# Batch 0's keys and queries laid out in two halves of head pairs, with padding written by memset and batch 1's query split placed between the first maxima

## The chip, the cores and the metric

The kernel runs on one core of a Trainium2 chip, as one program in which five engines work from their own queues and meet only through semaphores: TensorE (PE, with its weight loads PEld), VectorE (DVE), ScalarE (ACT), GpSimd (POOL) and SyncE (SP, which here only issues DMAs). The metric is device time in microseconds. Before the change the median of three runs is 338.34 us (338.0 to 339.09).

## The reference, cut to what matters

Four layers on `x` [4, 256, 128] with a context `ctx` [4, 512, 64]: self-attention plus cross-attention, a routed mixture of experts, a second cross-attention, a second mixture.

```python
x = x + tanh(g_xattn[0]) * L0_xattn(layernorm(x), ctx)   # the change lies in here
x = x + tanh(g_ffn[0])   * L0_ffn(layernorm(x))          # 8 experts, top 2, limited capacity
x = x + tanh(g_xattn[1]) * L1_xattn(layernorm(x), ctx)
x = x + tanh(g_ffn[1])   * L1_ffn(layernorm(x))

def L0_xattn(x, c):                                      # H = 16 heads of width 8
    q, k, v = heads(x @ Wq + bq), heads(x @ Wk + bk), heads(x @ Wv + bv)
    y  = softmax(causal(q @ k.T / sqrt(8))) @ v          # 256 queries on 256 keys
    qc, kc, vc = heads(x @ Wcq + bcq), heads(c @ Wck + bck), heads(c @ Wcv + bcv)
    y += softmax(qc @ kc.T / sqrt(8)) @ vc               # 256 queries on 512 context keys
    return merge(y) @ Wp + bp
```

## The kernel before, in words

**Parts and products.** A head has width 8, so one product would fill 8 of TensorE's 128 rows. Each float32 query and key is therefore cut into three bfloat16 parts (high, middle, low; tile `parts`, one row for each of the 128 channels) and six products of parts are laid side by side in the rows of two tiles, `qcat` and `kcat` (128 rows x batch x 8 head pairs x columns). In these a group of 64 rows holds one head of a pair; row r of every eight rows holds product r for r = 0 to 5, rows 6 and 7 of every eight are padding: ones in `kcat`, and in `qcat` zeros with the maxima of the scores put into some of them later. Query columns are 256 self and 256 cross (QW = 512); key columns 256 self and 512 context (KW = 768). `every(cat, b, r)` names the 16 rows r, r + 8, ... of batch b. One DMA fills one product of one batch: 16 rows x 8 pairs from 128 rows of `parts`. The weights are permuted first (`permute`), so that the projected channels come out in the order (parity, channel, pair) in which these copies need them.

**The lead.** For batch 0 the order on VectorE is written by hand: statistics of x tiles 0 and 1, permuting the weights, normalising, statistics of tiles 2 and 3, then `split` of the context keys, the queries, the self keys (high part, rest, middle part, low part: four operations each), with normalisations between, and the query split of batch 1. GpSimd takes the power -0.5 of the variances (`rstd_group`, lines 668 and 669) for the tile groups (0,1), (2,3), (4 to 7), then makes 14 constants in a row, then subtracts for batches 1 to 3 (line 720 for the remainder, 727 for the low part), with ScalarE casting between (`take_high` line 820, `split_middle` line 817). The projections are `jobs`: ct and xt (transposes of context and x), q, k, ck (keys of the context), v, cv. TensorE computes job j into a PSUM bank, ScalarE copies it out in the same order. `unread_zeros` are filler products on TensorE that nobody reads.

**Pass 1** computes the score maxima: eight parts (batch, half of the head pairs) of 11 units each: 8 "cross" (line 1583), 2 "late" (1585), 1 "early" (1588). VectorE reduces each unit (line 1174, two banks of 512 columns). After part n the maxima are split in three (GpSimd `split_max`, lines 710 to 713), turned by TensorE (1548), copied (1152) and brought into `qcat` by DMAs (`max_rows`, line 600). **Pass 2** computes the scores again with the maxima subtracted (lines 1607 to 1612), exponentiates on ScalarE (911) and multiplies by the values (1641). The first 18 steps of pass 1 run ahead of pass 2, each with one projection job behind it on TensorE.

**SyncE's queue** in order: the loads of x, context and weights; `pad(0)`; batch 0's context keys, three of the six query copies (ScalarE issues the other three), the self keys; seven small loads; `lay_out_batch(1)` and `pad(1)`; then for each part its `max_rows`, with batch 2 behind part 0's and batch 3 and the last pads behind part 1's.

## Time and profile before

| | us |
|---|---|
| median of 3 runs | 338.34 (338.0 to 339.09) |
| span of the profiled execution | 334.4 |
| PE busy in the span | 312.3 (93%) |
| DVE busy | 223.1 (67%) |
| ACT busy | 195.2 (58%) |
| POOL busy | 116.6 (35%) |
| first unit of pass 1 on TensorE | 19.50 |
| first scores of pass 2 on TensorE | 42.58 |

The profiled execution's time outside its span is not listed; the median of the runs stands 3.9 us above the span. The page's chain that ended last gives TensorE 67% of the span, VectorE 8%, SyncE's queue 5%, ScalarE 5%, GpSimd 5%. The granted TensorE clock has a mean of 1.00. In a timeline row stand start, length, engine, line, operation, output<-input, count, and in brackets the idle time ahead of it with what ended it; operations that follow one another on one line are merged, and a merged row's length runs from the first start to the last end.

### The profile page before, as it was taken

Reading aid. Unit: us, or ns where it says so; the run is one execution under the profiler, and the core shown is the slowest. Engines: PE = TensorE matmul, PEld = TensorE weight load, DVE = VectorE, ACT = ScalarE, POOL = GpSimd, SP = SyncE. Lnnn points to the kernel's source line nnn. Section 1 sums busy time; section 2 is a strip of 40 time slices with the busy share of each in tenths; the row PEclk is TensorE's granted clock in tenths of the full one; section 3 lists DMA queues with packets and bytes.
Section 4 is the critical chain, followed back from the end, with each engine's and each line's share of the span. In section 5 each row is a group of like instructions: output and inputs, shape, how many; then the busy total and the mean of one; then the engine's idle time right before and its main releaser. Section 6 shows DMA issues by size and latency. Waiting matters only on the chain.

```text
span 334.4 us, 7547 instructions
## 1 busy us (share of the span) xinstructions
PE 312.3 (93%) x2909; PEld 190.8 (57%) x2911; DVE 223.1 (67%) x537; ACT 195.2 (58%) x417; POOL 116.6 (35%) x209
## 2 busy tenths in 40 slices
PE   8778969989999999999989999999997899999995
PEld 3435733444444444354478677777795367676665
DVE  4998798888989898866544052333331957779665
ACT  3448588888889988867468633323336256422221
POOL 6476732325532343214477103444442211110000
PEclk9999999999999999999999999999999999999999
DMA  7956895950419005160081372000003100000101
GB/s 171 207 110 165 173 214 124 210 102 3 161 45 274 7 2 154 41 194 1 18 236 41 94 210 66 20 18 22 20 13 92 50 2 0 3 0 0 33 1 31
DMA packets 35827, 27.83 MB, mean 83 GB/s; under 512 B 5627, under 2 KB 33070, under 8 KB 35792
## 3 DMA queue, kind: packets, MB, share of 16 engines
q1 hardware_dynamic: 33965, 25.04, 30.0%
q0 software_dynamic: 1280, 1.88, 1.8%
q10 hardware_dynamic: 547, 0.44, 0.5%
q8 instruction: 23, 0.38, 0.5%
q14 instruction: 12, 0.10, 0.1%
HBM read 11.89 MB, written 5.26 MB: 51 GB/s over the span
## 4 chain that ended last, share of the span: by engine, by line
PE 67%; DVE 8%; SPq 5%; ACT 5%; POOL 5%; issue 5%; DMA 3%; DVEq 0%; ACTq 0%; POOLq 0%
PE psum L1835 11%; PE psum L1641 10%; PE psum L1916 8%; PE psum L1904 4%; PE psum L1823 4%; PE psum L1583 4%; PE psum L1607 3%; DVE nmax L1174 2%; SPq L544 2%; PE psum L1659 2%; POOL rows_in L773 2%; PE psum L2019 2%; PE psum L1610 2%; PE psum L2011 1%; PE psum L1773 1%
## 5 line engine op out<-in xcount | busy, mean ns | idle before, releaser
L1174 DVE TENSOR_REDUCE nmax<-psum 128x2 f32<-128x1024 f32 (+2 forms) x88 | 103.1, 1213 | 13.1 <-PE psum L1583 8.4
L911 ACT ACTIVATE parts<-psum 128x512 f32<-128x512 f32 (+1 forms) x88 | 45.2, 568 | 8.4 <-PE psum L1607 8.0
L1835 PE MATMUL psum<-p_more,kcat 128*128 128x320 f32 (+2 forms) x160 | 40.2, 396 | 0.9 <-DVE p_more L1305 0.7
L795 POOL DMA_INDIRECT rows_back<-qcat,back_at x24 | 22.9, 953 | 46.3 <-ACT qcat L944 40.3
L1835 PEld LDWEIGHTS psum<-p_more,kcat 128*128 128x128 f32 x160 | 26.1, 190 | 9.1 <-issue 0.9
L1309 DVE TENSOR_TENSOR qcat<-psum,qk_r 128x320 f32<-128x320 f32 (+2 forms) x40 | 16.7, 422 | 21.1 <-ACT qk_r L952 21.0
L952 ACT ACTIVATE qk_r<-psum 128x320 f32<-128x320 f32 (+2 forms) x40 | 15.3, 384 | 24.1 <-PE psum L1835 22.8
L1641 PE MATMUL psum<-parts,v_aug 128*9 128x256 f32 (+1 forms) x352 | 28.2, 366 | 0.0
L1916 PE MATMUL psum<-h_t,kcat 128*128 128x512 f32 x60 | 28.1, 594 | 0.0
L1641 PE MATMUL psum<-qk_r,v_aug 128*9 128x256 f32 (+1 forms) x160 | 27.1, 370 | 0.0
L990 ACT ACTIVATE qk_r<-psum 128x512 f32<-128x512 f32 x15 | 9.0, 597 | 30.1 <-PE psum L1916 30.1
L1583 PE MATMUL psum<-kcat,qcat 64*128 64x512 bf16 x128 | 24.9, 386 | 1.7 <-DMA qcat<-parts 1.7
L1607 PE MATMUL psum<-qcat,kcat 64*128 64x256 bf16 x256 | 24.7, 271 | 1.9 <-ACT p_more L911 0.8
L1641 PE MATMUL psum<-qk,v_aug 128*9 128x256 f32 (+1 forms) x160 | 25.8, 360 | 0.0
L1305 DVE COPY p_more<-psum 128x320 f32<-128x320 f32 x8 | 3.9, 492 | 28.1 <-PE psum L1813 28.1
L911 ACT ACTIVATE qk_r<-psum 128x512 f32<-128x512 f32 (+1 forms) x40 | 20.8, 574 | 2.0 <-PE psum L1607 1.8
L911 ACT ACTIVATE qk<-psum 128x512 f32<-128x512 f32 (+1 forms) x40 | 20.0, 551 | 1.9 <-PE psum L1607 1.9
L1583 PEld LDWEIGHTS psum<-kcat,qcat 64*128 64x128 bf16 x128 | 6.1, 92 | 24.4 <-issue 12.6
L1904 PEld LDWEIGHTS psum<-kcat,qcat 128*128 128x128 f32 x120 | 15.6, 191 | 6.4 <-issue 5.0
L773 POOL DMA_INDIRECT rows_in<-h_rows,put_at x16 | 15.9, 996 | 7.3 <-issue 4.4
L934 ACT ACTIVATE kcat<-psum 128x512 f32<-128x512 f32 x24 | 12.6, 616 | 8.3 <-PE psum L1773 8.3
L1358 DVE TENSOR_TENSOR qcat<-psum,qk_r 128x512 f32<-128x512 f32 x15 | 10.3, 690 | 9.5 <-ACT qk_r L990 9.5
(247 smaller groups left out, 627.2 us busy)
## 6 DMA issues: line engine op xcount, KB each, us to landing
kcat<-parts SPq DMA_DIRECT2D x18, 192.0 KB, 3.8
qcat<-parts SPq DMA_DIRECT2D x21, 128.0 KB, 3.6
kcat<-ones_b SPq DMA_DIRECT2D x8, 192.0 KB, 4.7
kcat<-in_L_ffn_wi_gate_dram SPq DMA_DIRECT2D x6, 256.0 KB, 4.3
kcat<-in_L_ffn_wi_up_dram SPq DMA_DIRECT2D x6, 256.0 KB, 4.6
kcat<-in_L_ffn_wo_dram SPq DMA_DIRECT2D x6, 256.0 KB, 5.4
parts<-in_L_ffn_w_dram SPq DMA_DIRECT2D x3, 512.0 KB, 5.5
rows_in<-zeros SPq DMA_DIRECT2D x1, 1290.0 KB, 6.2
```

The lines of the kernel that those rows point to most:

```text
L773: pool.indirect_dma_start(out=rows_in[0:E * SLOTS, :], out_offset=bass.IndirectOffsetOnAxis(ap=put_at[:, k, t:t + 1], axis=0), in_=h_rows[ ...
L795: pool.indirect_dma_start(out=rows_back[:, :], out_offset=bass.IndirectOffsetOnAxis(ap=back_at[0:m, e, t:t + 1], axis=0), in_=eo[0:m, e % ...
L911: act.activation(p_slots[u % NPT][:, 0:w], s2_bank(s2_place[u])[:, 0:w], ACT.Exp, scale=SCALE).then_inc(p_in, 1)
L952: act.activation(sg[:, i % 2, 0:m], gate_up_bank(i, 0)[:, 0:m], ACT.Silu).then_inc(sg_in[0], 1)
L1174: dve.tensor_reduce(dst[:, :, n * g:n * (g + 1)], src.rearrange("p (r q k) -> p r q k", r=PAR, q=n), AX.X, ALU.max, negate=True).then_inc( ...
L1309: dve.tensor_tensor(hh[:, e % 2, f, first:end], gate_up_bank(i, 1)[:, 0:end - first], sg[:, i % 2, 0:end - first], ALU.mult).then_inc(hh_i ...
L1583: ins = pe.matmul(dst, q[:, S + t * P:S + (t + 1) * P], k[:, S:KW], start=True, stop=True)
L1607: ins = pe.matmul(dst[:, c * S:(c + 1) * S], k[:, key:key + P], q[:, S:QW], start=True, stop=True)
L1641: ins = pe.matmul(bank(o_bank(n))[32 * j:32 * j + HA, cols], v_aug[:, v, h, :], p, start=r in (0, 2), stop=r in (1, ROUNDS - 1), skip_grou ...
L1835: ins = pe.matmul(gate_up_bank(i, m)[:, 0:end - first], w_t[e][:, m, f * P:(f + 1) * P], xs_t[:, e % 2, first:end], start=True, stop=True)
L1904: ins = pe.matmul(bank(DN_BANK[n % 4])[:, t * P:(t + 1) * P], hh1[:, n % 2, t * P:(t + 1) * P], w1_t[:, e, 2, :], start=True, stop=True)
L1916: ins = pe.matmul(bank(2 + 2 * (i % 2) + m), w1_t[:, e, m, :], h_t[:, s * BANK:(s + 1) * BANK], start=True, stop=True)
```

## The change

Batch 0's head pairs are laid out in two halves: pairs 0 to 3 first (all that part 0 of pass 1 reads), pairs 4 to 7 behind them, 18 copies of their own. For this batch 0 needs another channel order, (half, row, pair), so its weights are permuted by VectorE into a place of their own (`w_first`, `b_first`, inside `p_more`), and GpSimd permutes once more, in the order (row, pair), for batches 1 to 3. The padding of batch 0 is no longer copied by DMA: GpSimd sets the whole of batch 0's `kcat` to ones and VectorE the whole of its `qcat` to zeros before the copies. The statistics of tiles 2 and 3 move behind the split of the context keys. The query split of batch 1 is cut in two and stands behind the second and the fourth unit of pass 1 on VectorE; the clearing of bank 7 goes behind the fourteenth. `pad(1)` and the value weights are issued early on SyncE, and half of batch 1's copies go behind part 0's `max_rows`.

```diff
@@ sync @@
-            def lay_out_batch(b):
+            def lay_out_batch(b, first, end):
                 sp.wait_ge(parts_in, b + 1)
...
             sp.wait_ge(zero_in, 2)
-            pad(0)
+            pad(1)
+            sp.dma_start(w_v[:, :], a["L0_xattn_Wv"]).then_inc(in_wv, 16)
+            sp.dma_start(w_cv[0:DC, :], a["L0_xattn_Wcv"]).then_inc(in_wv, 16)
+            sp.dma_start(w_cv[DC:DC + 1, :], a["L0_xattn_bcv"].unsqueeze(0)).then_inc(in_wv, 16)
+            sp.wait_ge(ones_set, 1)
             sp.wait_ge(early_in, 1)
-            for dst, src in lay_out_k(0, S, KW):
+            for dst, src in first_k(0, S, KW):
                 sp.dma_start(dst, src).then_inc(cat_in[0], 16)
             sp.wait_ge(early_in, 2)
-            for dst, src in list(lay_out_q(0))[:Q_ON_SP]:
+            for dst, src in list(first_q(0))[:Q_ON_SP]:
                 sp.dma_start(dst, src).then_inc(cat_in[0], 16)
             sp.wait_ge(parts_in, 1)
-            for dst, src in lay_out_k(0, 0, S):
+            for dst, src in first_k(0, 0, S):
                 sp.dma_start(dst, src).then_inc(self_in, 16)
+            for pieces in (first_k(1, S, KW), first_q(1), first_k(1, 0, S)):
+                for dst, src in pieces:
+                    sp.dma_start(dst, src).then_inc(second_in, 16)
...
-            lay_out_batch(1)
-            pad(1)
+            lay_out_batch(1, 0, NPROD // 2)
...
                 if n == 0:
-                    lay_out_batch(2)
+                    lay_out_batch(1, NPROD // 2, NPROD)
+                    lay_out_batch(2, 0, NPROD)
@@ gpsimd @@
             rstd_group(0, *groups_of(0)[0])
-            pool.wait_ge(h_in[0], QT)
+            pool.memset(kcat[:, 0].rearrange("p a n -> p (a n)").bitcast(F32), TWO_ONES).then_inc(ones_set, 1)
+            rstd_group(0, *groups_of(0)[1])
+            pool.wait_ge(in_wq, 16 * N_IN_WQ)
+            permute(b_perm[:, :], b_rows)
+            for m, w in enumerate((w_q, w_cq, w_k)):
+                permute(w_perm[:, m, :], w)
+            pool.wait_ge(in_wck, 16 * N_IN_WCK)
+            permute(w_perm[0:DC + 1, 3, :], w_ck)
+            pool.wait_ge(perm_in, 5)
             const(pool.memset(c_t[DC:DC + 1, SC:NC * P], 1.0))
-            for first, end in groups_of(0)[1:]:
-                rstd_group(0, first, end)
+            rstd_group(0, *groups_of(0)[2])
@@ vector @@
+            dve.memset(q_zero[:, 0:Q_SET], 0.0)
             dve.wait_ge(in_x[0], 16)
             statistics(0, 0, x_sb)
...
+            dve.memset(q_zero[:, Q_SET:PAIR * QW // 2], 0.0)
             normalise(0, 0, x_sb)
...
-            dve.wait_ge(in_x[1], 16)
-            statistics(0, 1, x_sb)
...
             split(0, QW + S, XW, False)
+            dve.wait_ge(in_x[1], 16)
+            statistics(0, 1, x_sb)
             normalise(0, 1, x_sb)
...
-            dve.wait_ge(job_act, taken_count(job_at("q", SPLIT_DVE)))
-            split(SPLIT_DVE, 0, QW, False)
...
+                if i == SPLIT_AFTER[0]:
+                    split_cast(SPLIT_DVE, 0, QW)
+                if i == SPLIT_AFTER[1]:
+                    split_rest(SPLIT_DVE, 0, QW)
+                if i == SPLIT_AFTER[2]:
+                    wait_taken(dve, max(j for j in range(len(jobs)) if job_bank[j] == O_BANK))
+                    dve.memset(bank(O_BANK), 0.0).then_inc(o_clear, 1)
@@ tensor @@
                 if kind == "xt":
+                    if i == 1:
+                        pe.wait_ge(perm_in, 1)
+                        pe.transpose(dst[:, S:S + 3], b_perm[:, :], ident[0:3, 0:3])
...
-                        pe.wait_ge(perm_in, 1)
-                    ins = pe.matmul(dst, w_perm[0:DC + 1, 3, :],
+                        pe.wait_ge(perm_first, 1)
+                    else:
+                        pe.wait_ge(perm_in, 5)
+                    ins = pe.matmul(dst, (w_perm if i else w_first)[0:DC + 1, 3, :],
...
                     pe.wait_ge(cat_in[b], 16 * 2 * NPROD)
-                    pe.wait_ge(pad_in[b], 16 * 4)
+                    if b > 0:
+                        pe.wait_ge(pad_in[b], 16 * 4)
+                    if part == 1:
+                        pe.wait_ge(second_in, 16 * 3 * NPROD)
```

`SPLIT_AFTER` is (1, 3, 13), counted from 0. On TensorE the projection of the context keys of batch 1 waits, before and after, for GpSimd's memset of `c_t` (semaphore `consts`, value 4), and GpSimd's low part of batch 1 waits for the end of the query split (`early_in`, value 3).

VectorE's queue from the first normalisation to the statistics of tiles 4 to 7, before (`w_ck`, `w_q`, ... are weights, `qk` and `qk_r` the float32 values and the remainder):

```order
L1086 TENSOR_SCALAR h_rows<-x_sb,ln_mv,ln_rstd 128x128 x2
L1067 COPY b_perm<-b_rows 3x128
L1067 COPY w_perm<-w_q 128x128
L1067 COPY w_perm<-w_cq 128x128
L1067 COPY w_perm<-w_k 128x128
L1078 BN_STATS ln_stats<-x_sb 128x6 x2
L1081 BN_AGGR ln_mv<-ln_stats 128x2 x2
L1105 CAST parts<-qk 128x512
L1106 TENSOR_TENSOR qk_r<-qk,parts 128x512
L1112 CAST parts<-qk_r 128x512
L1113 TENSOR_TENSOR parts<-qk_r,parts 128x512
L1086 TENSOR_SCALAR h_rows<-x_sb,ln_mv,ln_rstd 128x128 x2
```

The same stretch of VectorE's queue after the change, from the first weight copy on:

```order
L1108 COPY p_more<-b_rows 3x128
L1108 COPY p_more<-w_q 128x128
L1108 COPY p_more<-w_cq 128x128
L1108 COPY p_more<-w_k 128x128
L1160 CAST parts<-qk 128x512
L1161 TENSOR_TENSOR qk_r<-qk,parts 128x512
L1167 CAST parts<-qk_r 128x512
L1168 TENSOR_TENSOR parts<-qk_r,parts 128x512
L1119 BN_STATS ln_stats<-x_sb 128x6 x2
L1122 BN_AGGR ln_mv<-ln_stats 128x2 x2
L1127 TENSOR_SCALAR h_rows<-x_sb,ln_mv,ln_rstd 128x128 x2
```

The statistics pair has moved from ahead of the four split operations to behind them, directly ahead of the normalisation of the same tiles; the copies write to `p_more`.

GpSimd's queue over the three `rstd` groups, before:

```order
L668 TENSOR_SCALAR ln_rstd<-ln_mv 128x2
L669 TENSOR_TENSOR ln_rstd<-ln_rstd,half_neg 128x2
L678 MEMSET c_t 1x1536
L668 TENSOR_SCALAR ln_rstd<-ln_mv 128x2
L669 TENSOR_TENSOR ln_rstd<-ln_rstd,half_neg 128x2
L668 TENSOR_SCALAR ln_rstd<-ln_mv 128x4
L669 TENSOR_TENSOR ln_rstd<-ln_rstd,half_neg 128x4
```

GpSimd's queue over the same stretch after:

```order
L698 TENSOR_TENSOR ln_rstd<-ln_rstd,half_neg 128x2
L710 MEMSET kcat 128x3072
L697 TENSOR_SCALAR ln_rstd<-ln_mv 128x2
L698 TENSOR_TENSOR ln_rstd<-ln_rstd,half_neg 128x2
L706 COPY b_perm<-b_rows 3x128
L706 COPY w_perm<-w_q 128x128
L706 COPY w_perm<-w_cq 128x128
L706 COPY w_perm<-w_k 128x128
L706 COPY w_perm<-w_ck 65x128
L719 MEMSET c_t 1x1536
L697 TENSOR_SCALAR ln_rstd<-ln_mv 128x4
L698 TENSOR_TENSOR ln_rstd<-ln_rstd,half_neg 128x4
```

The memset of `kcat` stands where that of `c_t` stood; five copies and the memset of `c_t` now stand between the second and the third group.

## Rows read from the trace of the kernel before

**Rows 1.** Chain that ended last, 0 to 76 us: start, length, what

```profile
14.52 1.13 POOL ln_rstd L669
...
21.24 1.65 POOL qk_r L720
...
51.49 0.78 SPq L600
...
67.07 0.77 SPq L600
```

**Rows 2.** VectorE's timeline, 0 to 46 us

```profile
1.18 0.27 DVE L1090 MEMSET zeros<- 128x258 f32 x1
...
3.69 0.25 DVE L1081 BATCH_NORM_AGGREGATE ln_mv<-ln_stats 128x2 f32<-128x6 f32 x2
...
5.11 0.61 DVE L1086 TENSOR_SCALAR h_rows<-x_sb,ln_mv,ln_rstd 128x128 f32<-128x128 f32 x2 [1.02 <-POOL ln_rstd L669]
5.62 0.25 DVE L1067 COPY b_perm<-b_rows 3x128 f32<-3x128 f32 x1
...
7.17 0.49 DVE L1078 BATCH_NORM_STATS2 ln_stats<-x_sb 128x6 f32<-128x128 f32 x2 [0.77 <-DMA x_sb<-in_x_dram]
...
10.07 0.60 DVE L1086 TENSOR_SCALAR h_rows<-x_sb,ln_mv,ln_rstd 128x128 f32<-128x128 f32 x2
...
11.04 0.69 DVE L1106 TENSOR_TENSOR qk_r<-qk,parts 128x512 f32<-128x512 f32 x1
...
12.84 0.86 DVE L1078 BATCH_NORM_STATS2 ln_stats<-x_sb 128x6 f32<-128x128 f32 x4
13.74 0.38 DVE L1081 BATCH_NORM_AGGREGATE ln_mv<-ln_stats 128x2 f32<-128x6 f32 x4
...
17.23 0.77 DVE L1106 TENSOR_TENSOR qk_r<-qk,parts 128x512 f32<-128x512 f32 x1
...
19.94 8.08 DVE L1174 TENSOR_REDUCE nmax<-psum 128x2 f32<-128x1024 f32 x7 [0.16 <-PE psum L1583]
```

**Rows 3.** ScalarE's timeline, 0 to 46 us: the context keys of batch 0

```profile
6.56 0.60 ACT L871 ACTIVATE qk<-psum 128x512 f32<-128x512 f32 x1 [1.22 <-PE psum L1519]
```

**Rows 4.** TensorE's timeline, 0 to 45 us

```profile
13.05 1.02 PE L1519 MATMUL psum<-c_t,w_perm 65*128 65x512 f32 x2
...
16.75 0.44 PE L1498 MATMUL psum<-ident,h_rows 128*128 128x128 f32 x2 [1.38 <-DVE h_rows L1086]
...
19.50 0.39 PE L1583 MATMUL psum<-kcat,qcat 64*128 64x512 bf16 x2 [1.67 <-DMA qcat<-parts]
...
27.05 1.10 PE L1509 MATMUL psum<-h_t,w_perm 128*128 128x256 f32 x4 [0.85 <-ACT h_t L850]
...
33.70 0.40 PE L1574 MATMUL psum<-mask_w,ident_w 64*128 64x128 bf16 x8
...
37.26 0.29 PE L1548 MATMUL psum<-ident_w,nmax_p 128*48 128x128 bf16 x2
```

**Rows 5.** GpSimd's timeline, 0 to 46 us

```profile
2.43 0.74 POOL L662 MEMSET ones_b<- 128x768 bf16 x1
...
5.77 1.95 POOL L678 MEMSET c_t<- 1x1536 f32 x1 [0.70 <-DVE h_rows L1086]
...
15.98 0.29 POOL L682 CAST ident_w<-ident 128x128 bf16<-128x128 f32 x1
...
23.83 1.64 POOL L727 TENSOR_TENSOR parts<-qk_r,parts 128x768 bf16<-128x768 f32 x1 [0.95 <-ACT parts L817]
...
26.71 2.61 POOL L720 TENSOR_TENSOR qk_r<-qk,parts 128x1280 f32<-128x1280 f32 x1 [1.24 <-ACT parts L820]
```

**Rows 6.** SyncE's queue, 0 to 78 us

```profile
16.03 3.92 SPq L556 DMA_DIRECT2D kcat<-parts  x6
...
47.26 0.61 SPq L544 DMA_DIRECT2D kcat<-parts  x1
```

**Rows 7.** DMA issues, 0 to 45 us: count, KB each, us to landing

```profile
kcat<-parts SPq DMA_DIRECT2D x6, 64.0 KB, 2.9
```

## What is predicted, before the changed kernel was run

> **What bounds the kernel now.** I read the 40 slices and the granted clock first (1.00 from end to end, so TensorE runs at its 2.4 GHz level and the clock is no term here), then the chain that ended last over the first 76 us, then each engine's timeline over the same stretch. The change ends there: behind 76 us nothing is edited, and most of the chain is TensorE in step with its own queue, so a shift at 76 us reaches the end nearly whole.
>
> In the chain [rows 1] the reader is to see that the lead is not bound by the first maxima. The path goes VectorE statistics of tiles 4 to 7 (end 14.12) -> GpSimd's rstd (ends 15.65) -> GpSimd's constants, without a gap -> GpSimd's first subtraction for batch 1 (21.24) -> ScalarE, whose projections of batch 2 stand behind the middle part of batch 1 -> TensorE's query projection of batch 3 at 27.05. From there TensorE has no gap in its timeline until past the first turn of the maxima at 37.26 [rows 4]; later the chain holds SyncE, issuing without a rest from 51.49 to 67.07. The first maxima start at 19.50 when the last query copy lands, 1.67 us after TensorE was ready. So an earlier landing alone pays nothing: the wait at 27.05 is made by GpSimd.
>
> **The change, part by part.**
>
> *Statistics moved behind the first split (VectorE).* From 7.17 to 14.12 VectorE worked without a gap: 6.95 us [rows 2]. The new order does the same work, but tiles 2 and 3 get their statistics directly ahead of their normalisation, so GpSimd's rstd is now waited for with nothing between. What that costs stands at the first group: statistics end 3.94, normalisation starts 5.11, 1.17 us. Before, the split hid it. In exchange VectorE need not wait for the x tiles at 7.17; the context keys are there at 7.1 [rows 3] and the copies are done at 6.40.
>
> *Padding by memset.* Two memsets of qcat on VectorE (1536 and 512 words): at 1.06 ns a word (258 words in 0.27 us [rows 2]) I estimate 1.6 and 0.55 us, which fall into its idle times ahead of the first statistics (1.45 to about 3.2, as 0.5 us of statistics stand ahead of the row at 3.69) and ahead of 5.11 (1.02 us), cost 0. The memset of kcat on GpSimd, 3072 words: 768 elements took 0.74 us [rows 5], four times that is 2.96, less three fixed parts, so 2.8 us, from 5.1 to 7.9. It starts as the first normalisation does, and ahead of VectorE's four weight copies (5.62 to 6.4). The question on which most hangs is who waits. GpSimd's 1536-word memset at 5.77 met these very copies and took 1.95 us; by the 768-element row it should take about 1.4, and the excess is near the 0.6 us of the copies: the two do exclude each other. The other way round there is one small row: a VectorE subtraction at 17.23, started while GpSimd had a select under way, took 0.77 us against 0.69 at 11.04 [rows 2]. Bounds: the copies are not held (0), or they are held until 7.9 (2.3 us). I take the second, since here GpSimd is first. Then the copies end at 8.7, and the split of the context keys starts at 8.7 instead of 7.1.
>
> The Trainium skill ("SBUF — State Buffer", Who interferes with whom) says that the port pair which VectorE's two-port copies and GpSimd share is locked for a whole instruction and that whoever comes first keeps it. The trace shows GpSimd as the loser, with 0.6 us; that VectorE loses for 2 us no row here shows. By that rule alone the sum is the one I take.
>
> *The sum to the statistics of tiles 4 to 7.* Held: 8.7 + 6.95 + 1.17 = 16.8. Not held: 7.1 + 6.95 + 1.17 = 15.2. Before: 14.12. So +2.7 or +1.1.
>
> *GpSimd behind it.* The second rstd ends 2.9 + 1.17 us after the split starts (7.17 to 10.07 is the 2.9): 12.8 held, 11.2 not. Then it has five new permuting copies (a contiguous 128x128 cast took 0.29 [rows 5]; with a gap 0.35 each, 1.7 us; strided they may cost twice that) and the 1536-word memset, 1.4 us, moved behind them; VectorE's casts (0.4 us, as between 10.67 and 11.04) hold them up, each once, 0.9 us taken. Together 4.0 us (bounds 3.1 to 6): 16.8 or 15.2, just when the statistics are there, so no more is added. Third rstd 1.5 us, constants 5.5 us as before (15.65 to 21.24), less some 0.2 since the batch 1 casts no longer meet them: the subtraction for batch 1 starts at about 23.8 or 22.2, +2.5 or +0.9.
>
> *Start of the maxima.* Half layouts carry half the bytes but are issued one for one: 0.65 us each [rows 6]. With the query split done 1.28 us before the statistics (12.84 to 14.12), the last query copy is issued 1.3 us later and lands about 2.9 us on for 64 KB [rows 7]: 19.7 or 18.1. But TensorE's context-key projection of batch 1 now waits for the memset that moved, until 16.8 or 15.2, and from it to the first maximum are 2.32 + 1.08 us of its own queue (13.05 to 15.37, 16.75 to 17.83 [rows 4]), plus the rstd wait of tiles 4 and 5 inside these: 20.3 or 18.7, against 19.50.
>
> *The batch 1 split between maxima.* About 2.3 us, as the same four operations took for batch 0 (10.6 to 12.84), leave VectorE before the maxima and come back in two halves behind the second and fourth. TensorE's seventh unit needs five reduces (8.08 / 7 = 1.154 each): 0.4 + 5 x 1.154 + 2.3 = 8.5 us after the first, and the unit itself takes 0.4, so the projection at 27.05 could go at about 29.2 or 27.6; GpSimd's road gives 29.55 or 27.95. Both ends meet. GpSimd's second subtraction for batch 1 (23.83 before) now waits for the fourth maximum and the rest of the split, 27.6 or 26.0, takes 1.64, and batch 2's (26.71) stands behind it: 29.3 or 27.7, so +2.6 or +1.0; GpSimd's road from there leads to the first turn of the maxima (37.26). I carry +2.6 and +1.1.
>
> *SyncE's queue.* Ahead of the first maximum of part 1 (33.70) now stand six self keys and eighteen second-half copies: from 18.3, 24 x 0.65, last landing 36.2 (33.3 + 2.9), where TensorE arrives at 33.70 + 2.5 = 36.2. Cost 0, up to 1 if one issue is long. Six batch 1 copies now follow the first row of maxima: SyncE was free at 47.87 and the next turn came at 51.49; 6 x 0.65 = 3.9 brings it to 51.75, both plus the shift: +0.3, and this is on the chain until 67.07.
>
> *At nothing:* the value weights loaded early (SyncE idled there), ones and zeros of batch 1 sent first, the second bias transpose (0.2 us on TensorE in its filler stretch), ScalarE's wait for the padding.
>
> Sum held: 2.6 + 0.3 = **+2.9 us**: span 334.4 to 337.3, and with the 3.9 us by which the median 338.34 stands above that span, 341.2. The profiled execution's own total isn't shown, so I hang the shift on the median.
>
> **Rivals.**
> 1. *GpSimd's memset gives way* and the copies run at 5.62. 1.1 + 0.3 = +1.4: 339.7 (339.2 to 340.6). For it: every large stretch in the trace is GpSimd's. Against: there it came second or had little to write.
> 2. *No measurable change.* The delay is eaten: the GpSimd constants run 0.6 shorter, and the SyncE term is nought; 338.0 to 339.3. Against: TensorE has no gap from 27.05 on.
> 3. *Faster.* The maxima start early and GpSimd reaches batch 1 before 21.24. It decides at the third rstd: it must start before about 14.2, that is, the 1.17 us must be hidden. Then at most the 0.85 us gap at 27.05 goes, 338.3 - 0.85 - 0.3 for shorter GpSimd constants: 337.2. Against: the wait is in the order of VectorE's own queue.
> 4. *Second halves late*: issues longer than 0.65 us or a landing beyond 2.9: +1 more, 342.3.
>
> **How the numbers follow.** Held 0.42, with late halves 0.08 (own range together 340.6 to 342.6); rival 1 0.27; no change 0.13; faster 0.10. Within 0.3% means 337.3 to 339.4, which takes a tenth of rival 1 too. So faster 0.10, same 0.17, slower 0.73. The range 339.2 to 342.5 leaves out the two last cases and a little above.
>
> **What would show it.** Held: the first weight copy on VectorE starts or ends near 7.9, not 5.8; the split of the context keys starts at 8.7. Either way: a gap of about 1.2 us ahead of the normalisation of tiles 2 and 3; GpSimd's first batch 1 subtraction after 22; TensorE's batch 3 query projection near 29.5 (held) or 28; SyncE busy without a gap from about 18 to 36 and again from 41 to 69. I am wrong if batch 1's subtraction starts by 21.3, or if a gap in TensorE's queue between 27 and 42 us swallows the delay.

## The result, and the profile after

The changed kernel takes 2.35% longer: the ratio to the kernel before is 1.0235, interval 1.0194 to 1.0276. A second comparison, on a chip where the kernel before takes about 345 us, gave 1.0261 (1.0213 to 1.0309). On the first ratio and 337.99 us for before in the first comparison, this is 345.9 us. The median as measured, 350.33 us, is no better number: three of the six runs took 345.0 to 346.3 us and three 354.3 to 354.9 at a lower granted clock, and before had only the first kind there. The profiled execution took 344.97 us, span 343.2 against 334.4: 8.8 us, where 2.9 were forecast.

The page of the changed kernel; digits are tenths, the clock's too:

```profile
span 343.2 us, 7577 instructions
PE 317.8 (93%) x2912; PEld 193.2 (56%) x2912; DVE 229.2 (67%) x539; ACT 195.7 (57%) x418; POOL 120.1 (35%) x215
...
PEclk9696999999999999999999999999999999999999
```

The clock was no term in the forecast. Here it falls twice inside the first 35 us, and nowhere else before the end.

VectorE of the changed kernel (start, length, what, and in brackets the idle time ahead with what ended it); it answers to [rows 2]:

```profile
5.09 2.72 DVE L1127 TENSOR_SCALAR h_rows<-x_sb,ln_mv,ln_rstd 128x128 f32<-128x128 f32 x2 [0.47 <-POOL ln_rstd L698]
7.74 0.25 DVE L1108 COPY p_more<-b_rows 3x128 f32<-3x128 f32 x1
...
8.44 0.41 DVE L1160 CAST parts<-qk 128x512 bf16<-128x512 f32 x1
...
11.19 0.25 DVE L1122 BATCH_NORM_AGGREGATE ln_mv<-ln_stats 128x2 f32<-128x6 f32 x2
12.59 0.78 DVE L1127 TENSOR_SCALAR h_rows<-x_sb,ln_mv,ln_rstd 128x128 f32<-128x128 f32 x2 [1.15 <-POOL ln_rstd L698]
...
23.68 1.81 DVE L1147 CAST parts<-qk 128x512 bf16<-128x512 f32 x1
25.52 0.69 DVE L1148 TENSOR_TENSOR qk_r<-qk,parts 128x512 f32<-128x512 f32 x1
26.25 2.36 DVE L1227 TENSOR_REDUCE nmax<-psum 128x2 f32<-128x1024 f32 x2
28.52 0.42 DVE L1153 CAST parts<-qk_r 128x512 bf16<-128x512 f32 x1
28.97 0.69 DVE L1154 TENSOR_TENSOR parts<-qk_r,parts 128x512 bf16<-128x512 f32 x1
```

GpSimd beside it, to [rows 5]:

```profile
5.01 2.66 POOL L710 MEMSET kcat<- 128x3072 f32 x1
...
23.57 1.64 POOL L760 TENSOR_TENSOR qk_r<-qk,parts 128x768 f32<-128x768 f32 x1
29.81 1.64 POOL L767 TENSOR_TENSOR parts<-qk_r,parts 128x768 bf16<-128x768 f32 x1 [4.61 <-DVE parts L1154]
31.40 2.60 POOL L760 TENSOR_TENSOR qk_r<-qk,parts 128x1280 f32<-128x1280 f32 x1
```

Two things of VectorE end only just after one of GpSimd's, though no semaphore joins them: the normalisation at 7.81, the memset at 7.67 (2.72 us, 0.61 before), and the cast at 25.49, the subtraction at 25.21 (1.81, the next one 0.42). Batch 2's subtraction starts at 31.40, 4.7 us later than before.

TensorE over the same stretch, to [rows 4]:

```profile
20.98 0.39 PE L1653 MATMUL psum<-kcat,qcat 64*128 64x512 bf16 x2
...
27.53 0.39 PE L1653 MATMUL psum<-kcat,qcat 64*128 64x512 bf16 x2 [1.90 <-DVE nmax L1227]
...
30.86 0.61 PE L1653 MATMUL psum<-kcat,qcat 64*128 64x512 bf16 x2 [0.59 <-DVE nmax L1227]
31.39 2.07 PE L1574 MATMUL psum<-h_t,w_perm 128*128 128x256 f32 x4
```

The projection of batch 3 comes 4.3 us late and takes 2.07 us, not 1.10. Last, ScalarE, and the chain from SyncE's last copy of batch 2 to it:

```profile
62.65 1.08 ACT L952 ACTIVATE parts<-psum 128x512 f32<-128x512 f32 x2 [3.27 <-DMA kcat<-parts]
```

```profile
44.66 0.86 SPq L628
...
56.27 0.61 SPq L569
56.92 5.71 DMA kcat<-parts
62.65 1.08 ACT parts L952 x2
```

ScalarE writes its exponentials where batch 2's split keys and queries lie, so it must wait until these are copied out. Before, the last of the copies was issued at 47.26 [rows 6] and nobody waited; now it is the row at 56.92, issued 9.7 us later, and it lands 5.7 us on.

So the 8.8 us stand in two places. The start of the second pass (the first scores for the exponentials, once the first maxima rows have landed) goes from 42.58 to 48.49: 5.9. From its fifth step on it is 3 us more (64.77 against 55.85): the 3.27 of ScalarE's wait. The ninth step is at 79.65 against 71.40, which is 8.25, since the kernel before waits there for a row of maxima (4.6 us from its eighth step, 4.0 after the change). From 167 us on the two are 8.6 to 8.8 apart.

### The profile page after: what moved, and what is told of

Read it like the earlier page. It is cut to its first block, busy times and chain, and to the rows that moved or that the text cites. A ratio compares the mean times of both kernels' runs of the same rounds, so it can differ in the third digit from the quotient of the medians.

```text
span 343.2 us, 7577 instructions
## 1 busy us (share of the span) xinstructions
PE 317.8 (93%) x2912; PEld 193.2 (56%) x2912; DVE 229.2 (67%) x539; ACT 195.7 (57%) x418; POOL 120.1 (35%) x215
## 4 chain that ended last, share of the span: by engine, by line
PE 64%; DVE 11%; POOL 6%; ACT 5%; DMA 5%; issue 5%; SPq 3%; DVEq 0%; ACTq 0%; POOLq 0%
PE psum L1711 11%; PE psum L1905 11%; PE psum L1986 8%; POOL rows_in L813 4%; PE psum L1653 4%; PE psum L1974 4%; PE psum L1893 4%; PE psum L1677 4%; SPq L569 3%; DVE nmax L1227 3%; PE psum L1729 2%; ACT parts L952 2%; PE psum L2089 2%; DVE h_rows L1127 2%; PE psum L1680 2%
## 5 line engine op out<-in xcount | busy, mean ns | idle before, releaser
L1653 PE MATMUL psum<-kcat,qcat 64*128 64x512 bf16 x128 | 25.6, 396 | 2.6 <-DVE nmax L1227 2.6
L1677 PEld LDWEIGHTS psum<-qcat,kcat 64*128 64x128 bf16 x256 | 10.6, 94 | 13.0 <-ACT parts L952 4.3
```

Source lines behind the costliest of these rows:

```text
L1653: ins = pe.matmul(dst, q[:, S + t * P:S + (t + 1) * P], k[:, S:KW], start=True, stop=True)
L1677: ins = pe.matmul(dst[:, c * S:(c + 1) * S], k[:, key:key + P], q[:, S:QW], start=True, stop=True)
```

## The experiments

Chips differ, so the table gives places in each profiled execution, in us, and the ratio to before on the same chip where there is one. Behind the first comparison four more were made, each on its own chip: of copies_back, split_back, ones_by_dma and all_three (the kernel before took 343.5 us there at the least); of after_repeat, before_repeat, stats_alone and shared_alone (343.6); of memset_alone and mended (336.4); of mended_whole and before_qset (335.8). The only traces of the kernel before are the first and before_repeat. "Norm. 2" is the start of VectorE's second normalisation, "stats" the end of the statistics of tiles 4 to 7, "b2" GpSimd's subtraction for batch 2, "turn" the first turn of the maxima, "pass 2" and "9th" the first and ninth step of the second pass.

| kernel | norm. 2 | stats | b2 | turn | pass 2 | 9th | ratio |
|---|---|---|---|---|---|---|---|
| before | 10.07 | 14.12 | 26.71 | 37.26 | 42.58 | 71.40 | 1 |
| before_repeat | 10.83 | 15.37 | 27.98 | 38.53 | 43.85 | 73.17 | |
| changed | 12.59 | 17.17 | 31.40 | 43.17 | 48.49 | 79.65 | 1.0235 |
| after_repeat | 12.40 | 17.00 | 31.25 | 43.53 | 48.85 | 79.97 | 1.0261 |
| copies_back | 12.63 | 17.21 | 31.44 | 42.98 | 49.70 | 79.88 | |
| split_back | 12.57 | 17.16 | 29.75 | 40.25 | 45.57 | 77.62 | 1.0114 |
| all_three | 11.52 | 16.11 | 28.70 | 39.23 | 52.40 | 83.32 | |
| stats_alone | 12.09 | 16.14 | 28.74 | 39.29 | 44.60 | 73.77 | 1.0064 |
| shared_alone | 10.05 | 14.09 | 29.56 | 39.98 | 45.82 | 75.12 | 1.0092 |
| memset_alone | 11.90 | 15.94 | 28.53 | 39.08 | 44.39 | 73.26 | 1.0022 |
| mended | 11.01 | 15.58 | 28.19 | 38.70 | 44.02 | 76.66 | 1.0120 |
| mended_whole | 11.03 | 15.61 | 28.21 | 38.71 | 44.03 | 72.72 | 1.0005 |
| before_qset | 10.19 | 14.24 | 28.87 | 39.41 | 44.73 | 73.45 | 0.9975 |

**Undoing one part of the change.** Three edits of the changed kernel, and all of them together. With the split the clearing of bank 7 goes back too.

```
copies_back:  -lay_out_batch(1, 0, NPROD // 2)       +lay_out_batch(1, 0, NPROD)
              -lay_out_batch(1, NPROD // 2, NPROD)    (behind the first maxima row)
split_back:   +split(SPLIT_DVE, 0, QW, False)         (ahead of the maxima, as before)
              -split_cast(...)  -split_rest(...)       (between the maxima)
ones_by_dma:  -pool.memset(kcat[:, 0]..., TWO_ONES)
              -pad(1) at the front   +pad(1) behind batch 1's first copies
              +sp.dma_start(every(kcat, 0, r), ones_b[:, :])   for the two rows
all_three:    the three together
```

> All six copy pairs of batch 1 stand ahead of the first row of maxima on SyncE again; everything else as in the changed kernel. Theory (three separate prices): in the changed kernel SyncE idles from 40.3 to 44.7 us, the six moved copies then push batch 2's last copy to a landing at 62.6, and ScalarE waits 3.3 us for it (its exponentials overwrite batch 2's parts). The moved copies fit into the idle time, so that wait goes or falls under 0.5 us, pass 2 still starts near 48.5, and the kernel takes 342.3 us (fast runs of the changed one: 345.6). Rival (the halves themselves cost, 18 copies more in the queue and on the DMA engines): ScalarE's wait stays above 2 us and the time at 345 to 346.

> The query split of batch 1 and the clearing of bank 7 stand ahead of the first maxima on VectorE again. Theory: GpSimd's 768-column subtraction (23.6 to 25.2) no longer holds a VectorE cast for 1.4 us between two maxima, TensorE's gaps of 1.9 us at 27.5 and 0.6 at 30.9 go, and with them the fall of the granted clock to 0.52 in 30 to 35 us; pass 2 starts at 45.5 to 46.5 instead of 48.5, ScalarE's wait for batch 2's copies stays, the kernel takes 343 us. Rival (the loss between maxima is only the moved 2.3 us, and moving it back puts the same 2.3 us ahead of the first maximum): pass 2 still at 48 to 48.5, 345 to 346 us.

> The ones of batch 0 come by two DMAs (as before the change) instead of GpSimd's memset of 3072 words; the zeros are still set by VectorE; the last pads of batch 1 go behind its first six copies. Theory: VectorE's first normalisation takes 0.6 us instead of 2.7, the context-key split starts at 7.1 instead of 8.4, TensorE's clock stays above 0.9 in 5 to 15 us, the statistics of tiles 4 to 7 end near 15.0 instead of 17.2, pass 2 starts near 46, and the kernel takes 343 us. Rival (VectorE's lateness comes from the moved statistics and the new copies on GpSimd, not from the memset): pass 2 at 48 and 345 us or more.

> The three edits together, so that what is left of the change is the halves, the two channel orders, the moved statistics and the early pads and weights. Theory: the prices are nearly independent, pass 2 starts at 43.5 to 44, no ScalarE wait, clock 1.00 throughout, 339 us, 1.0 to 1.4 us above the kernel before for the exposed rstd wait. Rival (the halves cost): pass 2 at 45 or later and 341 us or more.

split_back did what it should: turn and second pass 2.9 us earlier, ScalarE's wait as before (3.19). Its ratio, 1.0114 (1.0039 to 1.019), is against 1.0235 on the first chip. In copies_back ScalarE's wait is gone, but the first row of maxima now stands behind the six copies in SyncE's queue, and TensorE waits for it:

```profile
49.70 0.28 PE L1679 MATMUL psum<-qcat,kcat 64*128 64x256 bf16 x2 [1.77 <-DMA qcat<-nmax_t]
```

In all_three the turn is early, at 39.23, yet TensorE waits 8.2 us, because SyncE reaches the row only at 47.08, behind all twelve copies of batch 1 and the four of `pad(1)`; the second pass came at 52.40, not at the 43.5 to 44 that I expected:

```profile
46.43 0.61 SPq L563 DMA_DIRECT2D qcat<-zeros  x1
47.08 0.86 SPq L629 DMA_DIRECT2D qcat<-nmax_t  x1
```

ones_by_dma took the hold away (normalisation 0.60 us), but won only 0.66 us at the second normalisation, which went to 11.93, and the statistics ended at 16.52, not near 15.0. Its clock then stayed at half from 30 to about 65 us and its second pass began at 58.5, ratio 1.0617 (1.0511 to 1.0722); its times behind 27 us decide nothing.

The whole times of copies_back and all_three missed what I expected by far more: at the least 363.9 and 354.2 us, where I had 342.3 and 339. In both traces TensorE's clock is at about half from 200 to 220 us (0.53 and 0.50), far behind the edit, so these times price no part of the change, and no ratio stands for them.

**The same two kernels again, on a second chip.** Nothing is edited.

> The changed kernel, unedited, a second time, for a comparison with the kernel before on this chip and a second trace. If its two levels of time come from the kernel's own gaps (theory: VectorE's and GpSimd's holds in the lead, then a lowered TensorE clock), its trace has the same instruction starts up to the first lowered stretch: normalisation 2.7 us from 5.1, third unit of maxima held till about 23.6, second pass at 48 to 50, and ScalarE's 3.3 us wait on batch 2's last copy near 62. If the loss was that one chip's doing, the landmarks move back towards those of before (normalisation 0.61 us, second pass at 42.6) and the ratio falls to 1.00. Expected ratio 1.015 to 1.03.

> The kernel before, unedited, for a trace from this chip. Runs of it that are not profiled took from 343.5 to 359.1 us in the preceding comparison and 336.2 to 339.1 in the first. If the late lowered clock (between 180 and 225 us in three of the edited kernels, behind waits of TensorE ahead of the expert weights' transposes) belongs to the edits, this trace is at 2.4 GHz there; if it belongs to this chip, the same waits stand in it. The lead should be as in the first trace: second pass at 42.6 us.

The places of the changed kernel repeat within 0.4 us: the loss is the kernel's. The kernel before begins 1.3 us later here than in its first trace, since the two matmuls of TensorE's first context-key projection take 2.07 us together, not 1.13 (at a granted clock that still reads 1.00 there), and ScalarE's keys end at 8.54, not 7.16. So a single trace of the lead is good to about that; in shared_alone and before_qset, which have the same lead, the second normalisation starts at 10.05 and 10.19 as in the first trace. before_repeat also has late waits and a late fall of the clock (0.83 from 195 to 205 us) as the edited kernels do, so these don't need the change; a fall as deep as in all_three no trace of the kernel before shows.

```profile
186.13 3.10 PE L1774 MATMUL psum<-ident,parts 128*128 128x128 f32 x24 [2.01 <-issue]
```

**One part of the change alone, in the kernel before.**

```
stats_alone:   -dve.wait_ge(in_x[1], 16); statistics(0, 1, x_sb)   (ahead of the context keys' split)
               +the same two behind split(0, QW + S, XW, False)
shared_alone:  batch 1's split taken out ahead of the maxima and put behind maxima 1 and 3,
               counted from 0, as the changed kernel has it (bank 7 cleared behind the fourteenth)
memset_alone:  +link(pool.memset(kcat[:, 3]...[:, 0:3072], 0.0))   (behind the first rstd)
```

> The kernel before with one part of the change alone: the statistics of the second pair of tiles of batch 0 are moved behind the split of the context keys. Theory: the wait of 1.17 us for GpSimd's root, hidden behind the split before, stands open; the second normalisation goes from 10.07 to 11.2, the statistics of tiles 4 to 7 end at 15.2 instead of 14.12, the first unit of maxima at 20.3 instead of 19.5, and the second pass between 42.6 and 43.8. Rival: TensorE's own work there (the context transposes) covers it, and the maxima start at 19.5 unchanged.

> The kernel before with one part of the change alone: the split of batch 1's queries is taken out of its place ahead of the maxima and put in halves behind the second and the fourth maxima. Theory (splitting it there delays the chain of splits that TensorE's projections wait for): the first cast is held by GpSimd's subtraction or comes at 22 instead of 19, the q-projection of batch 3 goes from 27.05 to 29 to 30, the first turn from 37.26 to about 40, the second pass from 42.58 to about 45.5 (+2.9, as undoing it in the changed kernel took 2.9 off). Rival (it only costs behind a late lead): maxima start earlier, nothing is late, second pass within 0.5 of 42.58. As recorded ahead of the result: +2.6 at the turn.

> The kernel before with one thing added: behind its first root GpSimd fills 128 x 3072 words of kcat's fourth batch (which nobody reads before its own copies overwrite it) with zeros, in the place where the changed kernel has its memset of ones. Theory (held): VectorE's first normalisation lasts until the memset ends, 2.7 us instead of 0.61; the copies, the bias transposes and the q-projection of batch 0 move from 5.6, 6.1 and 7.5 to 7.7, 8.5 and 9.6; but the wait for ScalarE's eviction of the context keys ahead of the first split covers most of it, so the second normalisation is only 0.5 to 1 us late (10.6 to 11.1 instead of 10.07), the statistics of tiles 4 to 7 end at 14.7 to 15.1, GpSimd's own constants move with them, and the second pass starts 0.5 to 1.0 us late, at 43.1 to 43.6. As recorded (hold behind moved statistics): 1.6 us between held and not held. Rival (gives way): 0.6 us, nothing moves.

ScalarE's keys and VectorE of stats_alone:

```profile
7.22 0.60 ACT L871 ACTIVATE qk<-psum 128x512 f32<-128x512 f32 x1 [1.21 <-PE psum L1519]
```

```profile
7.85 0.43 DVE L1103 CAST parts<-qk 128x512 bf16<-128x512 f32 x1 [1.41 <-ACT qk L871]
...
10.62 0.25 DVE L1081 BATCH_NORM_AGGREGATE ln_mv<-ln_stats 128x2 f32<-128x6 f32 x2
12.09 0.60 DVE L1086 TENSOR_SCALAR h_rows<-x_sb,ln_mv,ln_rstd 128x128 f32<-128x128 f32 x2 [1.23 <-POOL ln_rstd L669]
```

The moved statistics cost 2.0 us in this trace, not the 1.2 that I expected, and the second pass came at 44.60, not by 43.8. The split starts at 7.85 in both traces, but for two reasons. Here it waits for ScalarE's keys, which end at 7.82. In the first trace of before they end at 7.16 [rows 3], and the split stands behind the statistics till 7.85. So in their old place the statistics cover keys that come up to 0.7 us late; moved, their own 0.8 us count, and the 1.23 us wait besides. With keys at 7.16 that is about 1.3 us (an estimate: 2.0 less the 0.7 that the keys came later), with keys at 7.82 it is 2.0. The ratio, 1.0064 (1.004 to 1.0087), is 2.2 us (1.4 to 3.0): about the whole shift reaches the end. The clock is 1.00 in this trace up to 180 us.

shared_alone, VectorE and GpSimd:

```profile
22.59 0.42 DVE L1107 CAST parts<-qk 128x512 bf16<-128x512 f32 x1
...
27.12 0.69 DVE L1114 TENSOR_TENSOR parts<-qk_r,parts 128x512 bf16<-128x512 f32 x1
```

```profile
20.50 1.64 POOL L721 TENSOR_TENSOR qk_r<-qk,parts 128x768 f32<-128x768 f32 x1
27.96 1.64 POOL L728 TENSOR_TENSOR parts<-qk_r,parts 128x768 bf16<-128x768 f32 x1 [5.82 <-DVE parts L1114]
29.56 2.61 POOL L721 TENSOR_TENSOR qk_r<-qk,parts 128x1280 f32<-128x1280 f32 x1
```

GpSimd's first subtraction is even 0.7 us earlier than before, and it gains nothing: it waits 5.8 us for VectorE's second half. +2.85 at batch 2, +3.2 at the second pass, ratio 1.0092 (1.005 to 1.0134), which is 3.2 us (1.7 to 4.6). In this trace the clock is at half from 20 to 25 us, so the 2.85 is not the sharing's alone. before_qset, further down, has the split in its old place and the same stretch at half clock, and its batch 2 subtraction comes at 28.87, 2.2 us late as well:

```profile
28.87 2.61 POOL L721 TENSOR_TENSOR qk_r<-qk,parts 128x1280 f32<-128x1280 f32 x1 [3.28 <-ACT parts L821]
```

In shared_alone VectorE stood idle for 0.9 us between its first four reduces, waiting for scores that TensorE computed at the low clock, which leaves about 2 us for the sharing (an estimate from those gaps). That it costs something in the kernel before rests on the ratio, and by it the rival, that it costs only behind a late lead, falls.

memset_alone shows the hold by itself, and a second one behind it:

```profile
5.05 2.72 DVE L1087 TENSOR_SCALAR h_rows<-x_sb,ln_mv,ln_rstd 128x128 f32<-128x128 f32 x2 [1.01 <-POOL ln_rstd L669]
...
9.06 1.01 DVE L1106 CAST parts<-qk 128x512 bf16<-128x512 f32 x1
...
11.90 0.60 DVE L1087 TENSOR_SCALAR h_rows<-x_sb,ln_mv,ln_rstd 128x128 f32<-128x128 f32 x2
```

It cost 1.8 us at the second normalisation and at the second pass, against the first trace of before from another chip, more than the 0.5 to 1 I expected. 1.2 us are the copies' delay (the split starts at 9.06, not 7.85), and 0.6 come from a second hold: GpSimd's other memset, one partition of 1536 words, now runs from 7.90 to 9.78 and holds the cast (1.01 us, 0.39 before). The ratio, 1.0022 (0.9992 to 1.0052), bounds the whole at 1.8 us and doesn't tell it from none.

**The changed kernel mended, with the halves and without.**

```
mended:        +pool.wait_ge(h_in[0], QT)             (ahead of the memset of ones)
               statistics(0, 1, x_sb) back ahead of the split; split_back's edit
mended_whole:  as mended, with lay_out_k(0, ...), lay_out_q(0) for first_k(0, ...), first_q(0);
               -for pieces in (first_k(1, S, KW), first_q(1), first_k(1, 0, S))
               VectorE permutes as before; and copies_back's edit
```

> The changed kernel with its three VectorE and GpSimd edits mended and its layout in halves kept: GpSimd's memset of ones waits for the first normalisation, the statistics of the second pair of tiles are back ahead of the context keys' split, batch 1's queries are split ahead of the maxima. The six copies of batch 1 stay behind the first maxima rows. Theory (the lead's loss is these three): normalisation 0.61, second normalisation at 10.1 to 10.9, statistics of tiles 4 to 7 end at 14.1 to 15.0, second pass at 42.6 to 43.6, five to six us earlier than in the changed kernel; ScalarE's 3 us wait on batch 2's last copy stays, since SyncE's eighteen more copies stay, so the whole is 2 to 4 us over before on this chip, ratio 1.005 to 1.012. Rival (the halves themselves are what costs): second pass at 46 or later. Rival (the halves bring something): first maxima before 19.3 and the ratio under 0.997.

> The mended kernel of the preceding run with batch 0 laid out whole again: every copy of batch 0 takes 128 partitions, the eighteen second-half copies are gone from SyncE's queue, and the six copies of batch 1 are back ahead of the first maxima rows. Kept are the memsets in place of batch 0's padding, GpSimd's copies of the weights and the early loads of the value weights. Theory (the halves' eighteen copies on SyncE are the rest of the loss): ScalarE's wait of 3.4 us on batch 2's last copy is gone, the second pass still begins at 43 to 44.5 and without a wait on the maxima rows, the ninth step of the second pass at 72 to 73.5 instead of 76.7, the ratio to before 0.998 to 1.005 where mended had 1.012. Rival (the wait comes from batch 1's late copies or from the shared traffic, not from the number of copies): the wait stays over 2 us, or one of more than 1 us appears ahead of the second pass, and the ratio stays at 1.01. The first unit of maxima may come later than 19.4, since whole copies take 2.9 to 3.8 us to land where halves took 1.9 to 2.1: at 19.5 to 20.5.

Mended, the second pass starts at 44.02, 4.5 us earlier than in the changed kernel but behind the 43.6 that I had at the latest (the later memset now holds a cast for 1.22 us), and the ratio is still 1.012 (1.0067 to 1.0172), because ScalarE's wait stays:

```profile
58.28 1.09 ACT L953 ACTIVATE parts<-psum 128x512 f32<-128x512 f32 x2 [3.38 <-DMA kcat<-parts]
```

With batch 0 laid out whole it is gone, at the same second pass to 0.01 us:

```profile
55.19 1.09 ACT L948 ACTIVATE parts<-psum 128x512 f32<-128x512 f32 x2 [0.28 <-PE psum L1668]
```

The ninth step is 3.9 us earlier and the ratio 1.0005 (0.9975 to 1.0035). This edit takes away the eighteen second-half copies and moves the six of batch 1 at once. copies_back moved the six alone, and there ScalarE's wait went too, but the row of maxima came late in its place: with eighteen copies more in the queue, one of the two waits stays in every run that keeps the halves. The first maximum came at 19.37 with the halves and at 20.30 without, and both kernels reached the turn at 38.70: the halves do bring the maxima forward, and that is worth nothing. SyncE's queue tells why whole copies suffice; in mended_whole batch 1 is out by 35.7 us, four us ahead of the row of maxima, where in mended only six of its twelve copies were:

```profile
35.10 0.61 SPq L568 DMA_DIRECT2D kcat<-parts  x1
39.62 0.86 SPq L624 DMA_DIRECT2D qcat<-nmax_t  x1
```

**The hidden part by itself.** The kernel before, with the padding of batch 0's queries filled by VectorE in place of two copies.

```
 before_qset:  -pad(0)   +its two copies of ones alone
               +dve.memset(q_zero[:, 0:Q_SET], 0.0) and the rest behind the first weight copy
```

> The kernel before with the one part of the change that stood in no busy stretch: the padding of batch 0's queries is filled by two VectorE memsets ahead of the first statistics (1.34 us) and behind the first copy of the weights (0.48 us), in place of two of the four padding copies on SyncE's queue; GpSimd gets no memset. Theory (both are hidden): same lead as before, second pass at 42.6 to 43.9, ratio 0.997 to 1.001; a gain only if 256 KB less traffic lets x and ctx land sooner. Rival (the memset runs into the first statistics): the first root and all behind it 0.1 to 0.3 us later, ratio 1.001 to 1.003.

The memsets took 1.34 and 0.48 us inside VectorE's idle times and the second normalisation began at 10.19. In this trace the clock is at half from 20 to 25 us and the second pass comes at 44.73, outside what I expected; its batch 2 subtraction is the row shown beside shared_alone. The ratio is 0.9975 (0.9944 to 1.0006): nothing that can be told from no change. No version was found that beats the kernel before.

## Why the prediction was wrong

The sign was right, at 0.73, and for the reasons given: the hold, the open wait, SyncE's queue. The size was not: +2.9 forecast, 8.8 measured, and 345.9 us lies outside the range of 339.2 to 342.5. Two terms of the sum were mis-sized and one was put at nothing. "Both ends meet", +2.6 up to the first turn of the maxima, measured 5.9, of which 1.2 is the clock, "no term here". SyncE's queue, +0.3, measured 3.0 net at the fifth step of the second pass.

**The memset holds VectorE.** Right. The normalisation ended just behind it and the weight copies started at 7.74 (forecast 7.9); I had thought of the copies as the ones held, but the normalisation itself was. The Trainium skill ("SBUF — State Buffer", Who interferes with whom) lists casts, copies and `tensor_scalar` among what can take the shared ports, and says that issue order decides; memset_alone agrees, with 2.72 us against 0.61.

**Sum to the statistics, 16.8.** Nearly right, at 17.17, and so were its shares. ScalarE's keys end at 7.01 in the changed kernel:

```profile
6.41 0.60 ACT L912 ACTIVATE qk<-psum 128x512 f32<-128x512 f32 x1 [1.22 <-PE psum L1586]
```

The split starts at 8.44 behind the held copies, so the hold cost 1.4 us (forecast 1.6). From there to the second normalisation it is 4.15 us, 1.9 more than before, less the 0.8 that the statistics no longer stand ahead of the split: 1.1 for moving them (forecast 1.1). The remaining 0.5 was no term: from 12.59 to 17.17 the same operations take 4.58 us, 4.05 before, beside GpSimd's five copies (normalisations 0.78 for 0.60, a cast 0.62 for 0.42); I had counted only what these copies lose. "In exchange VectorE need not wait for the x tiles" holds when the keys come early, as here. They end between 7.0 and 8.5 us in the traces, and without the hold a late landing counts in full: all_three, keys at 7.32, has the second normalisation at 11.52, ones_by_dma, keys at 7.73, at 11.93. GpSimd's first subtraction for batch 1 came at 23.57 (forecast 23.8).

**"Both ends meet", the split between maxima.** This is the first term that was mis-sized. I let VectorE's late second half and GpSimd's late constants cover one another, +2.6 together. GpSimd's batch 2 subtraction came 2.1 us after my 29.3: the cast held by GpSimd's own subtraction, 1.4 us, and maxima starting at 20.98 and not 20.3, 0.7. Starting from the changed lead, undoing the split won 1.65 us there; in the kernel before it cost about 2 besides the clock. It is a delay of its own, and the lead was delayed already.

**The clock is "no term here".** Wrong. In windows of the changed kernel (length; busy time and count of PE, weight load, DVE, ACT and POOL; granted clock; DMA share; GB/s):

```profile
5.00:10.00 5.00, 3.24 (x8) 1.57 (x9) 4.84 (x9) 1.31 (x4) 2.67 (x2) 0.74 1.13 237
10.00:15.00 5.00, 5.00 (x16) 2.71 (x15) 3.72 (x11) 1.31 (x3) 3.35 (x7) 0.57 0.55 129
...
25.00:30.00 5.00, 2.95 (x12) 0.99 (x10) 4.90 (x7) 3.97 (x7) 0.40 (x2) 0.79 0.30 104
30.00:35.00 5.00, 4.41 (x14) 1.94 (x14) 4.01 (x4) 2.09 (x4) 4.01 (x2) 0.52 0.21 62
```

```profile
7.80 0.69 PE L1561 MATMUL psum<-ident,h_rows 128*128 128x128 f32 x2 [1.43 <-DVE h_rows L1127]
```

TensorE waits 1.43 us for the held normalisation and 1.90 for VectorE between the maxima (till 27.53), and in these windows it runs at its 1.2 GHz level for some microseconds. That the waits bring the clock down is not shown: the first trace of before has waits of 1.38 and 1.67 us ahead of the first maxima [rows 4] and stays at 1.00, and before_qset, with 1.37 and 1.69, falls to 0.50 from 20 to 25 us. What does hold is that the changed kernel, after_repeat and copies_back all fall between 25 and 35 us, and split_back, with the split back in its place, does not. From batch 2's subtraction to the turn the changed kernel needs 11.77 us; before, split_back, shared_alone and stats_alone, all at full clock there, need 10.4 to 10.55. That is 1.2 us of clock, and with it the parts add up within these traces: 3.05 at the statistics (1.4 hold, 1.1 moved statistics, 0.5 beside GpSimd's copies), 1.65 for the split between maxima and 1.2 of clock are 5.9, as found.

**SyncE's queue: second halves 0, six copies +0.3.** The second term that was mis-sized. The halves did come in time, and TensorE did not wait for them. But I looked only at who waits for the maxima rows, and not at who waits for what stands behind. Six issues later, and 6.5 us later with the turn, batch 2's last copy is issued at 56.92 and lands at 62.6, and ScalarE wanted its room at 59.4. In the kernel before the same place had about 2.5 us to spare: last issue 47.26, DMA traffic over at about 51, room wanted at 53.5. So of the 11.5 us that the landing came later, 9.7 are SyncE's queue and the rest a later landing behind the issue (5.7 us for 3.8); 5.9 went with the second pass, 2.5 were spare, and about 3.3 are the wait. mended against mended_whole, on two chips, prices it, with all that the halves bring, at 0.0115 of the ratio, 3.9 us (about 1.8 to 6 by the two intervals).

**At nothing.** Right within what can be measured, about 1 us: mended_whole has GpSimd's copies, the early loads and the memsets in it, and its ratio is 1.0005. In its trace a cast held by the memset (1.31 us) and casts made longer by GpSimd's copies (0.62 for 0.42) do stand, and the second pass is 1.45 us behind the first trace of before, 0.2 behind the second one.

Of the rivals, the memset that gives way, no measurable change, the faster case and the late halves are excluded. My range was too narrow because its terms were joined by "the later of the two", each time with the smaller outcome.

Not settled: what makes the clock fall and how long it stays low once it has, which no run varied alone (ones_by_dma had it low for 35 us, the changed kernel for 5 to 10), and what TensorE waits for ahead of the experts' weights, behind 180 us, on some chips.

## What to carry to other kernels

When a piece of work is moved, first look whether it stood in a wait: then its own length counts at the new place besides any wait that it opens, and what it covered, such as keys that come late in some executions, lies open. When copies are put later in a queue, list everyone who waits for a landing behind them, those that want the source's room among them, and not only the reader of the destination. And a start that comes earlier (the first maxima, by 0.9 us) is worth nothing as long as another engine sets the next meeting.

## What the runs showed of the hardware

- A GpSimd memset of 128 x 3072 words took 2.66 us by itself and 3.24 us when it met VectorE's copies (mended). Under it an fp32 normalisation took 2.72 us for 0.61, and a 128x512 cast 1.22 for 0.39. Under a GpSimd subtraction the cast took 1.81. A VectorE subtraction beside GpSimd's work took 0.77 for 0.69.
- A VectorE memset of 1536 words took 1.34 us (0.87 ns a word), where 258 words took 0.27 and 512 took 0.48: my estimate from the small one was a fifth too high.
- An SBUF copy costs SyncE about 0.65 us from issue to issue, whether it moves 32, 64 or 192 KB; single ones took 1.1 to 1.8. Half copies landed in 1.9 to 2.1 us (32 and 64 KB, DMA share 0.2 to 0.6), whole ones of 128 and 192 KB in about 3.6 to 4.1. Size is not all of it: the copies of 64 KB in the kernel before took 2.9 us [rows 7], at a DMA share of 1.05. At a DMA share over 1 from 50 to 60 us, the last one took 5.7.
